# Down projection of the experts: weight columns held in TensorE, slots streamed, result transposed back before it is weighted

## Chip, cores and metric

The kernel runs on one core of one Trainium2 chip. The metric is the device time of one execution in microseconds (us). A core has a matrix engine (TensorE, PE), a vector engine (VectorE, DVE), a scalar engine (ScalarE, ACT), GpSimd (POOL), a queue for DMAs (SyncE, SP), and 16 DMA engines that all queues share. Each engine runs its own list of instructions in order and waits for the others at semaphores.

## What is computed

A tower of three parts: an edge filter on 32 images of 256 x 256, an attention block, and a mixture of experts. Only the last is touched. Its 8,224 tokens have 256 values each. Every token is routed to two of 32 experts, and an expert takes at most 321 tokens (its slots). Cut to what matters:

```python
idx = jnp.argsort(-score, axis=0)[:cap].T          # 32 experts x 321 slots
w = jnp.take_along_axis(Wc.T, idx, 1) * valid
xe = xf[idx]
up = jnp.einsum('eci,eji->ecj', xe, w_up)          # 256 -> 2 x 512
gate, upv = jnp.split(up, 2, axis=-1)
hact = jax.nn.silu(gate) * upv
ye = jnp.einsum('ecj,eoj->eco', hact, w_down)      # 512 -> 256
out = jnp.zeros((T, C), xf.dtype).at[idx.reshape(-1)].add((w[..., None] * ye).reshape(-1, C))
```

A small adapter (hidden width 128, one for two experts, factor 0.05) is added in the same way. The kernel appends it to the expert as a fifth block of 128 hidden values, so the down projection sums over 5 blocks.

## The kernel before

The expert stage is the last of the kernel. `body(n, r)` stands once per expert for each engine, with r = n mod 2 naming the buffer; experts 4 to 27 run in a loop of two bodies, the others are written out. All data are fp32; each operand is split into a high and a low part, and `mm3` (L243) makes one product from three matmuls (high x high, low x high, high x low). 322 slots (`CW`) are handled, in slot tiles of 128, 128 and 66 (`slot_tiles`, `ST` = 3).

For expert n the steps are:

- SP loads its weights into `raw` (L2078 up part, L2083 down part), once VectorE has finished with the buffer.
- ACT rounds them to `whi` in 4 pieces for the up part (`split_up`, L2190) and 2 for the down part (`split_down`, L2200), and VectorE makes the rest `wlo` (L2281).
- GpSimd gathers the token rows into `xe` (L2350, three indirect DMAs, one per slot tile). TensorE transposes them into `ps_f` (`turn`, L2151, six transpositions), ACT and VectorE make `xet` of it (L2220, L2298).
- `up(n, r, j)`, j = 0 to 4: 12 matmuls of 322 columns into `ps_s` (L247 to L249). ACT takes silu of one half (`gate`, L2180), VectorE multiplies it with the other (`hidden`, L2264 and L2266) and splits the product into `hs` (L2273, L2275).
- `down(m, r, st)`, one for each slot tile: the slots of `hs` are the stationary operand (128, 128 or 66 columns of it), the 256 weight columns stream through. 15 matmuls of 256 columns go into a bank of `ps_av`; its rows are slots. The tiles take the two banks in turn.
- `weigh` (L2211): ACT multiplies each row with the slot's weight and writes `ye`; GpSimd adds the rows into the output in HBM (L2366, an indirect DMA with add, one per slot tile).
- `row_weight` (L2288, L2289, L2291): three small VectorE instructions that make the slots' weights of expert n+1 in `weight[r]`. There are two such buffers, so it waits first:

```python
dve.wait_ge(xe_load[r], load_count(m, r, 16 * ST))
wait(dve, ye_done, ST * (m - 1))
```

With m = n+1 this is: all three weighings of expert n-1 are done. Behind it in VectorE's list stand the last piece of `wlo` of n+1 (`up_lo(n + 1, 1 - r, 3)`), for which `up(n + 1, r, 0)` waits on TensorE, and then the second down piece of n and `hidden` 4.

The down projection runs one expert late. TensorE's order in body n is: up 0, up 1, down tile 0 of n-1, up 2, down tile 1 of n-1, `turn` of n+1, up 3, down tile 2 of n-1, up 4. The last body (n = 32) has only `down_last`. GpSimd's order is fixed as well: for m = 0 to 31 the gathers of m+2, then the scatters of m. Hence the three gathers for n+2 stand behind the three scatters of n-1. They must have landed before `turn(n + 2)`, which TensorE reaches in body n+1.

Of the kernel before, what the change touches and what calls it, by code (L numbers as in the profile page):

```python
# [116 lines left out]
def build(nc, x, cls_rows, w1, b1uv, b1qk, w2, b2, gb, taps, r1w, r1s, r1m, r1b, r2w, wexp, consts, out,  # L117
# [9 lines left out]
    with ctx:  # L127
# [1894 lines left out]
        def s3(name, shape, dt=f32):  # L2022
            return experts.enter_context(nc.sbuf_tensor(name, shape, dt))
# [6 lines left out]
        xe = [s3(f"xe{i}", [P, ST, ROW]) for i in range(2)]  # L2030
        s3("over_raw", [P, POOL_COLS + 2 * WCOL - 4 * WCOL - 28 * CW - 2 * ST * ROW])
        ye = [s3(f"ye{i}", [P, ST, D]) for i in range(2)]
        sg = [s3(f"sg{i}", [P, CW]) for i in range(2)]
        hm = [s3(f"hm{i}", [P, CW]) for i in range(2)]
        weight = [s3(f"weight{i}", [P, ST]) for i in range(2)]
# [4 lines left out]


        w_hi_up, w_hi_dn, w_lo_up, w_lo_dn, xet_ps, xet_hi, xet_done = (sem(n) for n in ("w_hi_up", "w_hi_dn", "w_lo_up", "w_lo_dn", "xet_ps", "xet_hi", "xet_done"))
        up_ps, gate_act, h_done, h_hi, h_lo, down_ps, ye_done = (sem(n) for n in ("up_ps", "gate_act", "h_done", "h_hi", "h_lo", "down_ps", "ye_done"))
# [49 lines left out]
        def _(pe):  # L2093
# [17 lines left out]

            assert ST == 3

            def down_part(r, st, j0, j1):
                s0, w = slot_tiles[st]
                for j in range(j0, j1):
                    col = WDN + j * D
                    last = mm3(ps_av[(ST * r + st) % 2][0:w, 0:D], (hs[r][:, 0, j, s0:s0 + w], hs[r][:, 1, j, s0:s0 + w]),
                               (whi[r][:, col:col + D], wlo[r][:, col:col + D]), j == 0, j == 4)
                return last  # L2120

            def down(m, r, st):
                if not there(m):
                    return
                if st == 0:
                    pe.wait_ge(h_lo, 5 * m + 5)
                    pe.wait_ge(w_lo_dn, DNP * (m + 1))
                wait(pe, ye_done, ST * m + st - 1)
                down_part(r, st, 0, 5).then_inc(down_ps, 1)

            def down_last(m, r):

                pe.wait_ge(h_lo, 5 * m + 4)
                pe.wait_ge(w_lo_dn, DNP * (m + 1))
                wait(pe, ye_done, ST * m)
                down_part(r, 0, 0, 4)
                down_part(r, 1, 0, 4)
                pe.wait_ge(h_lo, 5 * m + 5)
                down_part(r, 0, 4, 5).then_inc(down_ps, 1)
                down_part(r, 1, 4, 5).then_inc(down_ps, 1)  # L2140
                pe.wait_ge(ye_done, ST * m + 1)
                down_part(r, 2, 0, 5).then_inc(down_ps, 1)

            def turn(m, r):
                if not there(m):
# [8 lines left out]
            def body(n, r):  # L2154
                if there(n):
                    up(n, r, 0)
                    up(n, r, 1)
                if isinstance(n, int) and n == NE:
                    down_last(n - 1, 1 - r)
                    return  # L2160
                down(n - 1, 1 - r, 0)
                if there(n):
                    up(n, r, 2)
                down(n - 1, 1 - r, 1)
                turn(n + 1, 1 - r)
                if there(n):
                    up(n, r, 3)
                down(n - 1, 1 - r, 2)
                if there(n):
                    up(n, r, 4)  # L2170

# [3 lines left out]
        def _(act):  # L2175
# [16 lines left out]
            def split_down(m, r, k):  # L2192

                if not there(m):
                    return
                if k == 0:
                    act.wait_ge(down_load[r], load_count(m, r, 16))
                    wait(act, down_ps, ST * (m - 1))
                lo, hi = dn_piece[k]
                nc.scalar.activation(whi[r][:, lo:hi], raw[r][:, lo:hi], ACT.Copy).then_inc(w_hi_dn, 1)  # L2200

            def weigh(m, r, st):
# [3 lines left out]
                if st == 0:  # L2206
                    act.wait_ge(w_ready, m + 1)
                    wait(act, added, 16 * ST * (m - 1))
                w = slot_tiles[st][1]
                act.wait_ge(down_ps, ST * m + st + 1)  # L2210
                nc.scalar.activation(ye[r][0:w, st, :], ps_av[(ST * r + st) % 2][0:w, 0:D], ACT.Copy,  # L2211
                                     scale=weight[r][0:w, st:st + 1]).then_inc(ye_done, 1)

            def turned_hi(m, r):
                if not there(m):
# [6 lines left out]
            def body(n, r):  # L2222
# [10 lines left out]
                if there(n):  # L2233
                    gate(n, r, 1)
                split_up(n + 1, 1 - r, 1)
                weigh(n - 1, 1 - r, 0)
                split_down(n, r, 0)
                if there(n):
                    gate(n, r, 2)
                split_up(n + 1, 1 - r, 2)  # L2240
                weigh(n - 1, 1 - r, 1)
                turned_hi(n + 1, 1 - r)
                if there(n):
                    gate(n, r, 3)
                split_up(n + 1, 1 - r, 3)
                weigh(n - 1, 1 - r, 2)
                split_down(n, r, 1)
                if there(n):
                    gate(n, r, 4)

# [3 lines left out]
        def _(dve):  # L2254
            def hidden(n, r, j):
# [4 lines left out]
                wait(dve, down_ps, ST * (n - 1))  # L2260
# [162 lines left out]
```

## Time and profile before

| what | value |
|---|---|
| median of 3 runs | 1458.1 us (1457.64 to 1460.12) |
| profiled execution | 1459.19 us, of which the span is 1457.4 us |
| mean granted TensorE clock | 0.936 of full speed |
| TensorE matmul busy | 1274.5 us (87% of the span) |
| VectorE busy | 1211.0 us (83%) |
| ScalarE busy | 892.6 us (61%) |
| GpSimd busy | 481.5 us (33%) |
| queue 1 (SP's loads and stores) | 153.80 MB, 35.9% of 16 engines' time |
| queue 0 (GpSimd's) | 21.25 MB, 9.1% |

The expert stage begins near 938 us with the first gathers and takes the rest of the span. The busy shares are means over all stages. What a step of the change is worth must be read from the order of events in one expert's period, and from what each engine waits for there. In the timelines a row is a start, a duration, the engine, the line, the operation and its operands; the duration of a matmul includes its way through the array, so matmuls follow each other faster than their durations say: the distance from start to start is the price. Brackets at the end of a row tell how long the engine was idle before, and who ended it.

### The profile page before, as it was taken

Reading aid. Unit: us, or ns where it says so; the run is one execution under the profiler, and the core shown is the slowest. Engines: PE = TensorE matmul, PEld = TensorE weight load, DVE = VectorE, ACT = ScalarE, POOL = GpSimd, SP = SyncE. Lnnn points to the kernel's source line nnn. Section 1 sums busy time; section 2 is a strip of 40 time slices with the busy share of each in tenths; the row PEclk is TensorE's granted clock in tenths of the full one; section 3 lists DMA queues with packets and bytes.
Section 4 is the critical chain, followed back from the end, with each engine's and each line's share of the span. In section 5 each row is a group of like instructions: output and inputs, shape, how many; then the busy total and the mean of one; then the engine's idle time right before and its main releaser. Section 6 shows DMA issues by size and latency. Waiting matters only on the chain. (4 is left out here: it accounts for less than half of the span.)

```text
span 1457.4 us, 33102 instructions
## 1 busy us (share of the span) xinstructions
PE 1274.5 (87%) x11891; PEld 1025.8 (70%) x11891; DVE 1211.0 (83%) x3133; ACT 892.6 (61%) x1608; POOL 481.5 (33%) x457
## 2 busy tenths in 40 slices
PE   3699999999999999999974342499999999999996
PEld 2467667667667667667653232399999999999996
DVE  4589999999999999999879878877777777777773
ACT  1377887887887887887772352545555555555552
POOL 0023233233233233232213000234554545555443
PEclk9799999999999999999996555699999999999999
DMA  8535445445445445442040600055565665655642
GB/s 243 136 94 133 112 116 133 111 116 133 110 118 133 112 116 133 113 116 58 31 145 17 93 0 0 20 189 153 163 191 152 179 178 148 188 169 150 198 123 24
DMA packets 128185, 176.69 MB, mean 121 GB/s; under 512 B 19946, under 2 KB 116476, under 8 KB 123964
## 3 DMA queue, kind: packets, MB, share of 16 engines
q1 hardware_dynamic: 110652, 153.80, 35.9%
q0 software_dynamic: 17408, 21.25, 9.1%
q8 instruction: 76, 1.25, 0.4%
q14 instruction: 49, 0.40, 0.1%
HBM read 133.85 MB, written 41.15 MB: 120 GB/s over the span
## 5 line engine op out<-in xcount | busy, mean ns | idle before, releaser
L796 ACT ACTIVATE at<-ps_s 128x1024 f32<-128x1024 f32 x256 | 248.3, 1027 | 5.5 <-PE ps_s L532 4.4
L2366 POOL DMA_INDIRECT out_rows<-ye,slot_token x96 | 152.3, 1587 | 227.2 <-ACT ye L2211 211.8
L247 PE MATMUL ps_s<-xet,whi 128*128 128x322 f32 x640 | 206.2, 322 | 11.0 <-DVE wlo L2281 9.5
L249 PE MATMUL ps_s<-xet,whi 128*128 128x322 f32 x640 | 199.4, 312 | 0.0
L248 PE MATMUL ps_s<-xet,wlo 128*128 128x322 f32 x640 | 198.9, 311 | 0.0
L2180 ACT ACTIVATE sg<-ps_s 128x322 f32<-128x322 f32 x160 | 70.5, 440 | 173.2 <-PE ps_s L249 132.9
L2281 DVE TENSOR_TENSOR wlo<-raw,whi 128x640 fp32r<-128x640 f32 x192 | 153.9, 817 | 2.3 <-ACT whi L2190 1.3
L2264 DVE TENSOR_TENSOR hm<-ps_s,sg 128x322 f32<-128x322 f32 x128 | 63.3, 494 | 98.8 <-ACT sg L2180 77.8
L548 PE MATMUL ps_av<-at,uv 128*16 128x257 f32 x2048 | 136.4, 384 | 1.0 <-ACT at L840 0.5
L247 PEld LDWEIGHTS ps_s<-xet,whi 128*128 128x128 f32 x640 | 121.7, 190 | 19.2 <-issue 15.7
L247 PE MATMUL ps_av<-whi,hs 128*128 128x256 f32 (+1 forms) x480 | 134.5, 280 | 0.6 <-issue 0.3
L248 PE MATMUL ps_av<-whi,hs 128*128 128x256 f32 (+1 forms) x480 | 134.5, 280 | 0.0
L249 PE MATMUL ps_av<-wlo,hs 128*128 128x256 f32 (+1 forms) x480 | 134.4, 280 | 0.0
L1527 POOL TENSOR_TENSOR rsa<-vea,n 128x2 f32<-128x2 f32 x32 | 22.3, 698 | 336.2 <-DVE vea L1042 336.2
L248 PEld LDWEIGHTS ps_s<-xet,wlo 128*128 128x128 f32 x640 | 121.6, 190 | 0.0
L249 PEld LDWEIGHTS ps_s<-xet,whi 128*128 128x128 f32 x640 | 121.6, 190 | 0.0
L2350 POOL DMA_INDIRECT xe<-token_rows,slot_token x96 | 102.9, 1072 | 30.2 <-issue 28.7
L532 PEld LDWEIGHTS ps_s<-qd,kd 32*128 32x128 f32 x2048 | 69.9, 185 | 44.2 <-issue 40.4
L532 PE MATMUL ps_s<-qd,kd 32*128 32x256 f32 x2048 | 96.1, 304 | 4.9 <-ACT at L796 2.5
L2190 ACT ACTIVATE whi<-raw 128x640 fp32r<-128x640 f32 x128 | 92.9, 731 | 11.9 <-PEq L2012 11.9
L2211 ACT ACTIVATE ye<-ps_av,weight 128x256 f32<-128x256 f32 (+1 forms) x96 | 45.3, 473 | 71.5 <-PE ps_av L249 70.8
L247 PE MATMUL ps_f<-xt,w1s 128*128 128x256 f32 x256 | 79.3, 310 | 6.1 <-DVE xt L1052 3.1
(393 smaller groups left out, 3556.5 us busy)
## 6 DMA issues: line engine op xcount, KB each, us to landing
raw<-in_wexp SPq DMA_DIRECT2D x32, 1280.0 KB, 6.4
halo<-gray_dram SPq DMA_DIRECT2D x96, 288.0 KB
xb<-in_x SPq DMA_DIRECT2D x64, 384.0 KB, 4.8
raw<-in_wexp SPq DMA_DIRECT2D x32, 640.0 KB
gray_dram<-g SPq DMA_DIRECT2D x32, 256.0 KB, 3.5
out_rows<-h SPq DMA_DIRECT2D x64, 128.0 KB, 3.3
token_rows<-xf SPq DMA_DIRECT2D x64, 128.0 KB, 2.5
pre_dram<-pre SPq DMA_DIRECT2D x30, 128.0 KB, 1.7
```

The source lines that it names most:

```text
L247: nc.tensor.matmul(o, lh, rh, start=first, stop=False)
L248: nc.tensor.matmul(o, ll, rh, start=False, stop=False)
L249: return nc.tensor.matmul(o, lh, rl, start=False, stop=last)
L532: last = nc.tensor.matmul(ps_s[j // 2][:, j % 2, kt, :], kd[r % 2][row, e, a, kt * 128:kt * 128 + 128], qd[r % 2][row, hl, e, a, :], start ...
L548: last = nc.tensor.matmul(o[32 * j:32 * j + 16, 0:R + 1], uv[r % 2][:, kt, 256 + h * 16:256 + h * 16 + 16], at[:, t, j, kt, 0:R + 1], star ...
L796: nc.scalar.activation(at[:, t, 2 * i:2 * i + 2, :, 0:R].rearrange("p j k q -> p (j k) q"), ps_s[i][:, :, :, :].rearrange("p j k q -> p (j ...
L2180: nc.scalar.activation(sg[b][:, :], ps_s[b][:, 0, :, :].rearrange("p k q -> p (k q)")[:, 0:CW], ACT.Silu).then_inc(gate_act, 1)
L2190: nc.scalar.activation(whi[r][:, lo:hi], raw[r][:, lo:hi], ACT.Copy).then_inc(w_hi_up, 1)
L2264: nc.vector.tensor_tensor(hm[b][:, :], o, sg[b][:, :], ALU.mult).then_inc(h_done, 1)
L2281: nc.vector.tensor_tensor(wlo[r][:, lo:hi], raw[r][:, lo:hi], whi[r][:, lo:hi].bitcast(f32), ALU.subtract).then_inc(done, 1)
L2350: nc.gpsimd.indirect_dma_start(out=xe[r][0:w, st, :], out_offset=None, in_=token_rows, in_offset=bass.IndirectOffsetOnAxis(ap=slot_token[0 ...
L2366: nc.gpsimd.indirect_dma_start(out=out, out_offset=bass.IndirectOffsetOnAxis(ap=slot_token[0:w, 3 * m + st:3 * m + st + 1], axis=0), in_=y ...
```

## The change

The roles in the down projection are exchanged. The weights become the stationary operand, 128 of their 256 output columns at a time (a half, `hf`), and all 322 slots stream through. That makes 2 x 15 matmuls of 322 columns per expert. Their result has output values as rows and slots as columns, so it cannot be weighted row by row. ACT first copies each half into a new SBUF tile `yt` (`keep_half`). TensorE turns it back with six transpositions into the same two `ps_av` banks (`back_rows`; two for each slot tile), and then ACT weighs as before.

In TensorE's order `down` 0 and 1 stand where tiles 0 and 1 stood, and `back_rows` where tile 2 stood. On ACT `keep_half` takes the places of weighings 0 and 1 (the first piece of `split_down` now stands ahead of it). All three weighings stand behind `gate` 3, `split_up` 3 and `split_down` 1. VectorE's and GpSimd's lists are the same. Nothing changes in the DMAs' sizes.

```diff
+        yt = s3("yt", [P, 2, CW])
...
-            def down_part(r, st, j0, j1):
-                s0, w = slot_tiles[st]
+            def down_part(r, hf, j0, j1):
                 for j in range(j0, j1):
-                    col = WDN + j * D
-                    last = mm3(ps_av[(ST * r + st) % 2][0:w, 0:D], (hs[r][:, 0, j, s0:s0 + w], hs[r][:, 1, j, s0:s0 + w]),
-                               (whi[r][:, col:col + D], wlo[r][:, col:col + D]), j == 0, j == 4)
+                    col = WDN + j * D + 128 * hf
+                    last = mm3(ps_av[hf][:, 0:CW], (whi[r][:, col:col + 128], wlo[r][:, col:col + 128]),
+                               (hs[r][:, 0, j, :], hs[r][:, 1, j, :]), j == 0, j == 4)
                 return last
 
-            def down(m, r, st):
+            def down(m, r, hf):
...
-                wait(pe, ye_done, ST * m + st - 1)
-                down_part(r, st, 0, 5).then_inc(down_ps, 1)
+                wait(pe, ye_done, ST * (m - 1) + 2 + hf)
+                down_part(r, hf, 0, 5).then_inc(down_ps, 1)
...
                 down_part(r, 0, 4, 5).then_inc(down_ps, 1)
                 down_part(r, 1, 4, 5).then_inc(down_ps, 1)
-                pe.wait_ge(ye_done, ST * m + 1)
-                down_part(r, 2, 0, 5).then_inc(down_ps, 1)
+
+            def back_rows(m):
+                if not there(m):
+                    return
+                pe.wait_ge(yt_done, 2 * m + 2)
+                for st, (s0, w) in enumerate(slot_tiles):
+                    for hf in range(2):
+                        last = nc.tensor.transpose(ps_av[st // 2][0:w, 256 * (st % 2) + 128 * hf:256 * (st % 2) + 128 * hf + 128],
+                                                   yt[:, hf, s0:s0 + w], ident)
+                    last.then_inc(back_ps, 1)
...
-                down(n - 1, 1 - r, 2)
+                back_rows(n - 1)
...
-                act.wait_ge(down_ps, ST * m + st + 1)
-                nc.scalar.activation(ye[r][0:w, st, :], ps_av[(ST * r + st) % 2][0:w, 0:D], ACT.Copy,
+                act.wait_ge(back_ps, ST * m + max(st + 1, 2))
+                nc.scalar.activation(ye[r][0:w, st, :], ps_av[st // 2][0:w, 256 * (st % 2):256 * (st % 2) + D], ACT.Copy,
                                      scale=weight[r][0:w, st:st + 1]).then_inc(ye_done, 1)
+
+            def keep_half(m, hf):
+
+                if not there(m):
+                    return
+                if hf == 0:
+                    wait(act, back_ps, ST * m)
+                act.wait_ge(down_ps, 2 * m + hf + 1)
+                nc.scalar.activation(yt[:, hf, :], ps_av[hf][:, 0:CW], ACT.Copy).then_inc(yt_done, 1)
...
-                weigh(n - 1, 1 - r, 0)
                 split_down(n, r, 0)
+                keep_half(n - 1, 0)
...
-                weigh(n - 1, 1 - r, 1)
+                keep_half(n - 1, 1)
...
-                weigh(n - 1, 1 - r, 2)
                 split_down(n, r, 1)
+                for st in range(ST):
+                    weigh(n - 1, 1 - r, st)
```

Where the instructions stand now. TensorE of the kernel before, at the end of up 3 and through the third tile's down projection to the start of up 4 (`ps_s` is up, `ps_av` is down):

```order
L247 MATMUL ps_s<-xet1,whi1 128x322
L248 MATMUL ps_s<-xet1,wlo1 128x322
L249 MATMUL ps_s<-xet1,whi1 128x322
L247 MATMUL ps_av0<-whi0,hs0 66x256 [waits ye_done]
L248 MATMUL ps_av0<-whi0,hs0 66x256
L249 MATMUL ps_av0<-wlo0,hs0 66x256
...
L247 MATMUL ps_s<-xet1,whi1 128x322 [waits h_done]
```

Four more such triples stand at the dots. The same place in the changed kernel:

```order
L247 MATMUL ps_s<-xet1,whi1 128x322
L248 MATMUL ps_s<-xet1,wlo1 128x322
L249 MATMUL ps_s<-xet1,whi1 128x322
L2149 MATMUL ps_av0<-cst,yt 128x128 [waits yt_done]
L2149 MATMUL ps_av0<-cst,yt 128x128 x3
L2149 MATMUL ps_av1<-cst,yt 66x128 x2
L247 MATMUL ps_s<-xet1,whi1 128x322 [waits h_done]
```

The 15 matmuls of the third tile have gone, and the six transpositions of `yt` stand between up 3 and up 4.

ScalarE of the kernel before, from `gate` 3 (`sg1`) to `gate` 4 (`sg0`) of one expert:

```order
L2180 ACTIVATE sg1<-ps_s 128x322 [waits h_done,up_ps]
L2190 ACTIVATE whi1<-raw1 128x640
L2210 REGISTER_ALU
L2211 ACTIVATE ye1<-ps_av1,weight1 66x256 [waits down_ps]
L2200 ACTIVATE whi0<-raw0 128x640
L2177 REGISTER_ALU
L2180 ACTIVATE sg0<-ps_s 128x322 [waits h_done,up_ps]
```

And in the changed kernel:

```order
L2190 ACTIVATE sg1<-ps_s 128x322 [waits h_done,up_ps]
L2200 ACTIVATE whi1<-raw1 128x640
L2210 ACTIVATE whi0<-raw0 128x640
L241 ISA [waits w_ready]
L2220 REGISTER_ALU [waits added]
L2221 ACTIVATE ye1<-ps_av0,weight1 128x256 [waits back_ps] x2
L2220 REGISTER_ALU
L2221 ACTIVATE ye1<-ps_av1,weight1 66x256 [waits back_ps]
L2187 REGISTER_ALU
L2190 ACTIVATE sg0<-ps_s 128x322 [waits h_done,up_ps]
```

All three weighings (`ye`) now stand behind both pieces of weights (`whi`); only the third stood between these two gates before, ahead of the down piece.

## Rows read from the trace of the kernel before

**Rows 1.** Timeline of GpSimd: scatters (`out_rows`) and gathers (`xe`), start and duration.

```profile
966.75 2.13 POOL L2366 DMA_INDIRECT out_rows<-ye,slot_token  x1 [14.33 <-ACT ye L2211]
...
1106.43 1.73 POOL L2366 DMA_INDIRECT out_rows<-ye,slot_token  x1 [2.66 <-ACT ye L2211]
...
1113.61 1.48 POOL L2366 DMA_INDIRECT out_rows<-ye,slot_token  x1 [2.59 <-ACT ye L2211]
1115.40 1.10 POOL L2350 DMA_INDIRECT xe<-token_rows,slot_token  x1 [0.30 <-issue]
...
1118.16 1.02 POOL L2350 DMA_INDIRECT xe<-token_rows,slot_token  x1 [0.30 <-issue]
...
1417.44 1.64 POOL L2366 DMA_INDIRECT out_rows<-ye,slot_token  x1 [2.63 <-ACT ye L2211]
...
1445.26 1.59 POOL L2366 DMA_INDIRECT out_rows<-ye,slot_token  x1 [4.59 <-ACT ye L2211]
...
1449.02 1.48 POOL L2366 DMA_INDIRECT out_rows<-ye,slot_token  x1 [0.30 <-issue]
```

**Rows 2.** Table by stretch: length, busy time per engine, PEclk, DMA share, GB/s.

```profile
1100.00:1200.00 100.00, 97.95 (x723) 96.21 (x722) 77.50 (x169) 52.15 (x104) 51.88 (x40) 1.00 0.63 181
...
1108.00:1109.00 1.00, 1.00 (x12) 1.00 (x11) 0.97 (x3) 0.31 (x1) 0.16 (x1) 1.00 0.45 19
...
905.00:910.00 5.00, 0.00 (x0) 0.00 (x0) 4.76 (x18) 0.00 (x0) 0.00 (x0) 0.56 0.00 2
...
1385.00:1390.00 5.00, 4.16 (x34) 3.95 (x33) 2.85 (x6) 2.26 (x5) 2.79 (x2) 1.00 0.42 70
...
1386.00:1386.50 0.50, 0.50 (x6) 0.49 (x5) 0.50 (x1) 0.02 (x1) 0.20 (x1) 1.00 0.12 41
```

**Rows 3.** Timeline of TensorE from `turn` to the next expert's first matmul.

```profile
1108.49 0.72 PE L2151 MATMUL ps_f<-cst,xe 128*128 128x128 f32 x6
1109.02 0.39 PE L247 MATMUL ps_s<-xet,whi 128*128 128x322 f32 x1
...
1110.88 0.28 PE L247 MATMUL ps_av<-whi,hs 128*66 128x256 f32 x1
...
1112.64 0.31 PE L247 MATMUL ps_s<-xet,whi 128*128 128x322 f32 x1
...
1114.27 0.31 PE L249 MATMUL ps_s<-xet,whi 128*128 128x322 f32 x1
1114.91 0.41 PE L247 MATMUL ps_s<-xet,whi 128*128 128x322 f32 x1 [0.33 <-DVE wlo L2281]
```

**Rows 4.** Timeline of VectorE: `row_weight` begins, and the last up piece follows.

```profile
1113.46 0.22 DVE L2288 SCALAR_TENSOR_TENSOR is<-xe,cst 128x3 f32<-128x3 f32 x1
...
1113.96 1.56 DVE L2281 TENSOR_TENSOR wlo<-raw,whi 128x640 fp32r<-128x640 f32 x2
```

**Rows 5.** Timeline of ScalarE: four pieces in a row, one expert, two weighings in a row.

```profile
939.78 2.60 ACT L2190 ACTIVATE whi<-raw 128x640 fp32r<-128x640 f32 x4
...
1111.08 0.44 ACT L2180 ACTIVATE sg<-ps_s 128x322 f32<-128x322 f32 x1 [1.26 <-PE ps_s L249]
1111.41 0.73 ACT L2190 ACTIVATE whi<-raw 128x640 fp32r<-128x640 f32 x1
1112.84 0.47 ACT L2211 ACTIVATE ye<-ps_av,weight 66x256 f32<-66x256 f32 x1 [0.70 <-PE ps_av L249]
...
1444.01 0.84 ACT L2211 ACTIVATE ye<-ps_av,weight 128x256 f32<-128x256 f32 x2 [3.40 <-PE ps_av L249]
```

**Rows 6.** Timelines of GpSimd and TensorE: third gather, and `turn` that waits for gathers.

```profile
942.26 1.18 POOL L2350 DMA_INDIRECT xe<-token_rows,slot_token  x1 [0.30 <-issue]
...
945.17 1.33 PE L2151 MATMUL ps_f<-cst,xe 128*128 128x128 f32 x6 [9.81 <-DMA xe<-token_rows,slot_token]
...
1380.88 1.02 POOL L2350 DMA_INDIRECT xe<-token_rows,slot_token  x1 [0.30 <-issue]
...
1387.53 0.78 PE L2151 MATMUL ps_f<-cst,xe 128*128 128x128 f32 x6 [0.84 <-DMA xe<-token_rows,slot_token]
```

**Rows 7.** DMA queues from 1000 to 1400 us: packets, MB, share of 16 engines.

```profile
q1 hardware_dynamic: 7394, 50.72, 32.8%
q0 software_dynamic: 14019, 17.01, 27.0%
```

More of the change, by code:

```diff
@@ L2042, in build @@
         w_hi_up, w_hi_dn, w_lo_up, w_lo_dn, xet_ps, xet_hi, xet_done = (sem(n) for n in ("w_hi_up", "w_hi_dn", "w_lo_up", "w_lo_dn", "xet_ps", "xet_hi", "xet_done"))
-        up_ps, gate_act, h_done, h_hi, h_lo, down_ps, ye_done = (sem(n) for n in ("up_ps", "gate_act", "h_done", "h_hi", "h_lo", "down_ps", "ye_done"))
+        up_ps, gate_act, h_done, h_hi, h_lo, down_ps, yt_done, back_ps, ye_done = (sem(n) for n in (
+            "up_ps", "gate_act", "h_done", "h_hi", "h_lo", "down_ps", "yt_done", "back_ps", "ye_done"))
         w_part, w_ready, added, tail_clear = (sem(n) for n in ("w_part", "w_ready", "added", "tail_clear"))
@@ L2112, in _ @@
             assert ST == 3
-            def down_part(r, st, j0, j1):
-                s0, w = slot_tiles[st]
+            def down_part(r, hf, j0, j1):
                 for j in range(j0, j1):
-                    col = WDN + j * D
-                    last = mm3(ps_av[(ST * r + st) % 2][0:w, 0:D], (hs[r][:, 0, j, s0:s0 + w], hs[r][:, 1, j, s0:s0 + w]),
-                               (whi[r][:, col:col + D], wlo[r][:, col:col + D]), j == 0, j == 4)
+                    col = WDN + j * D + 128 * hf
+                    last = mm3(ps_av[hf][:, 0:CW], (whi[r][:, col:col + 128], wlo[r][:, col:col + 128]),
+                               (hs[r][:, 0, j, :], hs[r][:, 1, j, :]), j == 0, j == 4)
                 return last
-            def down(m, r, st):
+            def down(m, r, hf):
                 if not there(m):
                     return
-                if st == 0:
+                if hf == 0:
                     pe.wait_ge(h_lo, 5 * m + 5)
                     pe.wait_ge(w_lo_dn, DNP * (m + 1))
-                wait(pe, ye_done, ST * m + st - 1)
-                down_part(r, st, 0, 5).then_inc(down_ps, 1)
+                wait(pe, ye_done, ST * (m - 1) + 2 + hf)
+                down_part(r, hf, 0, 5).then_inc(down_ps, 1)
             def down_last(m, r):
@@ L2134, in down_last @@
                 pe.wait_ge(w_lo_dn, DNP * (m + 1))
-                wait(pe, ye_done, ST * m)
+                pe.wait_ge(ye_done, ST * m)
                 down_part(r, 0, 0, 4)
@@ L2167, in body @@
                     up(n, r, 3)
-                down(n - 1, 1 - r, 2)
+                back_rows(n - 1)
                 if there(n):
@@ L2197, in split_down @@
                     act.wait_ge(down_load[r], load_count(m, r, 16))
-                    wait(act, down_ps, ST * (m - 1))
+                    wait(act, down_ps, 2 * (m - 1))
                 lo, hi = dn_piece[k]
@@ L2209, in weigh @@
                 w = slot_tiles[st][1]
-                act.wait_ge(down_ps, ST * m + st + 1)
-                nc.scalar.activation(ye[r][0:w, st, :], ps_av[(ST * r + st) % 2][0:w, 0:D], ACT.Copy,
+                act.wait_ge(back_ps, ST * m + max(st + 1, 2))
+                nc.scalar.activation(ye[r][0:w, st, :], ps_av[st // 2][0:w, 256 * (st % 2):256 * (st % 2) + D], ACT.Copy,
                                      scale=weight[r][0:w, st:st + 1]).then_inc(ye_done, 1)
+            def keep_half(m, hf):
+                if not there(m):
+                    return
+                if hf == 0:
+                    wait(act, back_ps, ST * m)
+                act.wait_ge(down_ps, 2 * m + hf + 1)
+                nc.scalar.activation(yt[:, hf, :], ps_av[hf][:, 0:CW], ACT.Copy).then_inc(yt_done, 1)
             def turned_hi(m, r):
@@ L2259, in hidden @@
                 dve.wait_ge(gate_act, 5 * n + j + 1)
-                wait(dve, down_ps, ST * (n - 1))
+                wait(dve, down_ps, 2 * (n - 1))
                 o = ps_s[b][:, 1, :, :].rearrange("p k q -> p (k q)")[:, 0:CW]
```

## The prediction

> **What bounds the kernel now.** I read the views in the order of the groups. The expert stage runs from 966 us to 1425 us with one expert after another: the first scatters of experts 0 and 29 start at 966.75 and 1417.44 us, 29 periods, so one period is 450.69/29 = 15.54 us [rows 1]. TensorE looks like the bound, 97.95 us busy of 100 at a granted clock of 1.00 [rows 2]. But it waits in every period: its last matmul of an expert starts at 1114.27, its first of the next at 1114.91, released by `wlo` of VectorE [rows 3]. So TensorE and a loop through VectorE are nearly level. In that loop `gate` 3 (ACT, 1111.08) lets VectorE make `hm`, split a piece, then do `row_weight` (1113.46) and the last up piece `wlo` (1113.96), and TensorE may begin [rows 4, 5]. `row_weight` of expert n+1 overwrites the row weights that expert n-1 used, so by its wait on `ye_done` it may not start before the third weighing of n-1. That one ran from 1112.84 to 1113.31, 0.15 us before `row_weight` started: it was just in time [rows 4, 5].
>
> A third loop runs through GpSimd. Its order is fixed: three scatters of expert n-1, then three gathers for n+2. The gathers must land before the transpositions of `turn` in the next expert. At 1387.53 TensorE sat waiting for just that, 6.65 us after the third gather's issue began at 1380.88 [rows 6]. That loop has next to no room either.
>
> I put all times of one expert relative to G, the start of `gate` 3 (1111.08 in these rows).
>
> **The change on TensorE.** Removed are 45 matmuls of 256 columns; 15 of them take 1112.64 - 1110.88 = 1.76 us, so 0.117 each and 5.28 us in all [rows 3]. Added are 30 of 322 columns; the up projection has this shape, 11 of them in 1114.27 - 1112.64 = 1.63 us, so 0.148 each and 4.44 us [rows 3]. The six transpositions back have the form of the six in `turn`, which take 1109.02 - 1108.49 = 0.53 us [rows 3]. Sum: 4.44 + 0.53 - 5.28 = -0.31 us per expert, 10 us in 32. For bounds I take 0.53 to 0.8 us for the six.
>
> The Trainium skill ("TensorE: Matmul & The Clock Gate", Part 4: PE-mode transpose) gives about 275 ns for one transposition in a kernel's context. By that six would cost 1.65 us and TensorE alone would be 0.8 us per expert slower. The trace speaks against it as a price in a row of them: six in 0.53 us.
>
> That saving is real but stands in the wrong place. Ahead of G, two tiles (30 x 0.117 = 3.52 us) become two halves (4.44 us): +0.92 us on every loop through G. Behind G, 1.76 us of the third tile become 0.53 us, and that stretch ended in a wait already. So all of the saving falls where TensorE waits anyway.
>
> **The change on ScalarE and VectorE.** Two copies `keep_half` are added, one of them in place of each of the first two weighings, which is where ACT waited anyway. They cost nothing while ACT waits there 0.7 us and more; with that cover gone, about 0.4 us each. All three weighings now stand behind `gate` 3, a piece of `split_up` and a piece of `split_down`. The up piece starts 0.33 us after the gate; pieces in a row follow each other by (2.60 - 0.73)/3 = 0.62 us, so the down piece starts at G + 0.95 and the first weighing at G + 1.57; two weighings in a row take 0.84 us, one 0.47, so they follow by 0.37 and the third starts at G + 2.31 and ends at G + 2.78 [rows 5]. The transpositions are done by about G + 0.8, so they are not what it waits for. `row_weight` follows by 0.03 to 0.15 us: G + 2.93 against 1113.46 - 1111.08 = 2.38 before, +0.55 us (bounds 0.43 and 0.6) [rows 4, 5]. Queued behind it on VectorE is the last up piece, and TensorE waits for that. The cover on TensorE behind G is 0.53 + 12 x 0.148 = 2.3 us, so the gap at the next expert's start grows from 0.3 to about 2.1 us. **This loop's period: 15.54 + 0.92 + 0.55 = 17.0 us.**
>
> **The change on GpSimd and its queue.** Before, the three scatters were spread over the period; only the third (1113.61, G + 2.5) stood close ahead of the gathers, whose third began at 1118.16 (G + 7.1) [rows 1]. Now all three wait for weighings behind G. The first weighing ends at G + 2.04. At the end of the kernel the weighing ended at 1444.48 and the first scatter began at 1445.26, 0.78 later; the third followed at 1449.02, 3.76 later [rows 1, 5]. So: first scatter G + 2.82, third G + 6.58, first gather 1.79 later (1115.40 - 1113.61), third gather another 2.76 later: G + 11.13, 4.0 us later than before [rows 1]. Then it lands after a time L, `turn` may start, and from there to the next G it is 1111.08 - 1108.49 = 2.59 us [rows 3, 5]. **This loop's period: 11.13 + L + 2.59 = 13.72 + L.**
>
> L is not shown for this order. Lower bound: 2.91 us with the queues nearly empty (942.26 to 945.17); upper bound: 6.65 us beside a whole load of weights [rows 6]. Between them I count the DMA engines' work. Weights and software queue take 32.8% and 27.0% of 400 us over 26 experts, 9.2 us of all 16 engines per expert [rows 7]. Before, two of the three scatters were issued before G, ahead of the weights. Now none is. A scatter's packets come about 2.1 us after its start (1106.43; the engines' share in 1108 to 1109 is 0.45 [rows 1, 2]), so from G + 4.95 everything runs in one piece: scatters, the weights that `wlo` releases, gathers last in their queue. They end at G + 4.95 + 9.2 = G + 14.15. At 1386 to 1386.5 the engines were down to 0.12 and TensorE started at 1387.53, so 1.4 us from the last packet to the wait's end [rows 2, 6]. `turn` starts at G + 15.55, which is L = 4.4, near the middle of the two rows. **Period 18.15 us**; that is more than 17.0, so this loop rules, 2.6 us per period over 15.54.
>
> **Sum.** 30 experts (1 to 30) have both a predecessor to scatter and a successor to prepare: 30 x 2.6 = 78 us. At the end the first scatter waits for both halves, a copy and the transpositions: 4.44 + 0.44 + 0.53 against 3.52 = +1.9 us. Together 80 us on the profiled execution's 1459.2 us (span 1457.4): 1539 us. The median of the runs is 1458.1, 1.1 lower, so 1538 us.
>
> **Rivals.**
> 1. *Only the VectorE loop counts* (gathers land in time). For it: L = 2.91 would give 16.6, under 17.0. Against it: three scatters, weights and gathers now meet in the DMA engines. Price 30 x 1.47 + 2 = 46 us: 1504 us. The Trainium skill ("DMA: Bandwidth & Descriptors", Anatomy of one DMA — SWDGE (gpsimd) path) prices such a DMA at 2.0 us plus its bytes over 436 GB/s; for 66 rows that is an estimate of 2.2 us and would put the case here. The trace shows 2.91 and 6.65 us. Chance 0.20.
> 2. *The queue is as slow as beside a full load*: L = 5.5 to 6.65, periods 19.2 to 20.4, 1570 to 1605 us. For it: in the rows with long L there were fewer scatters in the queue than now. Against it: the weights are issued about 4 us ahead of the first gather, so most of them are through. Chance 0.09 beyond the range.
> 3. *TensorE's own sum rules, faster*: the weights loop and the gathers turn out to have room, each period loses 0.31 us: 1448 us. It decides only if `row_weight` does not wait for the third weighing and the gathers not for the scatters. The waits stand in the code. Chance 0.04.
> 4. *The clock falls* in the new gaps (about 2.1 us at an expert's start, 1.1 at `turn`). With TensorE idle for all of 905 to 910 it was granted 0.56; around the 0.84 us wait before 1387.53 it was 1.00 [rows 2, 6]. If the 12 matmuls after one of the gaps ran at half speed it would be 1.8 us more per period, about 1590 us. Chance 0.03.
>
> **Chances and range.** My forecast, the GpSimd loop at 17.3 to 19.2 us per period (1513 to 1570 us), has 0.64. The range holds it and the first rival: 1498 to 1572 us. A measurement of this kernel can tell about 0.2% from no change; slower by more 0.94, faster by more 0.04, within 0.02 (taken from the lower end of rival 1).
>
> **What the profile after would show.** Scatters in threes 1.9 us apart, starting near G + 2.8, the third gather near G + 11; waits of 1 to 2 us of `turn` on the DMA of `xe` in most experts (if they are missing, rival 1 holds); the wait of an expert's first matmul on `wlo` at 1.5 to 2.2 us; 30 matmuls for the down projection at 0.148; clock 1.00. I would be wrong if scatter packets overlap with weights at little cost (then 1504 to 1520), or if ACT reached the weighings much earlier than G + 1.6.

## The result, and the profile after

The changed kernel takes 1519.4 us (median of 3 runs, 1518.14 to 1520.4) against 1458.1: ratio 1.0421, 95% interval 1.0407 to 1.0434. It is slower by 61 us; 80 were forecast. Its profiled execution has a span of 1518.6 us.

From the page of the changed kernel, to be read beside the page of before:

```profile
span 1518.6 us, 32669 instructions
...
PE 1279.4 (84%) x11603; PEld 1028.1 (68%) x11603; DVE 1221.8 (80%) x3133; ACT 908.4 (60%) x1672; POOL 486.7 (32%) x457
...
q1 hardware_dynamic: 110652, 153.80, 33.9%
q0 software_dynamic: 17408, 21.25, 7.8%
```

Where does one period begin and end? GpSimd's timeline of the changed kernel, one expert. It answers to [rows 1]. `gate` 3, my G, starts at 1114.98 here:

```profile
1109.48 1.02 POOL L2370 DMA_INDIRECT xe<-token_rows,slot_token  x1 [0.30 <-issue]
1117.86 1.64 POOL L2386 DMA_INDIRECT out_rows<-ye,slot_token  x1 [7.36 <-ACT ye L2221]
1119.80 1.60 POOL L2386 DMA_INDIRECT out_rows<-ye,slot_token  x1 [0.30 <-issue]
1121.71 1.49 POOL L2386 DMA_INDIRECT out_rows<-ye,slot_token  x1 [0.31 <-issue]
1123.51 1.10 POOL L2370 DMA_INDIRECT xe<-token_rows,slot_token  x1 [0.30 <-issue]
...
1126.38 1.02 POOL L2370 DMA_INDIRECT xe<-token_rows,slot_token  x1 [0.30 <-issue]
```

The three scatters now stand together, ahead of the three gathers. The first scatter starts at G + 2.88 and the third gather at G + 11.40. The first scatters of experts 0 and 29 start at 973.50 and 1483.36, so the mean period is 509.86/29 = 17.58 us, against 15.54 before. The shortest periods are 16.8 to 16.9; others go up to 18.9. The 29 periods account for 59.2 us of the 61.2 us between the two spans. The remaining 2.0 lie at the stage's two ends.

The stretches of [rows 2] again (columns as there: stretch, its length, busy time of the five engines, granted clock, share of the DMA engines, GB/s):

```profile
1082.00:1084.00 2.00, 0.15 (x2) 0.00 (x0) 1.51 (x6) 0.85 (x3) 1.36 (x1) 1.00 0.00 0
1084.00:1088.00 4.00, 3.86 (x16) 3.87 (x17) 2.27 (x4) 0.30 (x1) 3.34 (x3) 0.57 0.85 220
...
1100.00:1200.00 100.00, 87.84 (x601) 85.47 (x600) 72.96 (x154) 49.34 (x106) 48.03 (x36) 1.00 0.52 158
1000.00:1400.00 400.00, 348.90 (x2338) 339.27 (x2337) 283.23 (x596) 195.29 (x413) 183.76 (x138) 0.98 0.50 151
```

TensorE is busy for 87.84 of 100 us where it was 97.95 [rows 2]. The idle time is told by the list of waits of the changed kernel, 1000 to 1400 us (the engine and what it works on, what ended the wait; sum in us, count, longest; `PEld` is TensorE's loading of the stationary operand):

```profile
PE ps_s L247 <- DVE wlo L2301: 45.5, 23, 2.0
...
DVE is L2308 <- ACT ye L2221: 10.4, 23, 0.5
...
PEld ps_f L2160 <- DMA xe<-token_rows,slot_token: 8.7, 13, 1.5
...
PE ps_f L2160 <- DMA xe<-token_rows,slot_token: 5.6, 8, 1.3
```

The first line holds one wait of 1.98 us in each of 23 experts. That is the gap at an expert's start, 0.33 us in [rows 3]. The second shows why: `row_weight` now waits 0.45 us for the third weighing. The last two lines are `turn` waiting for gathers; on the matmul side it does so in 8 of 23 experts, by up to 1.3 us.

The order around G, which answers to [rows 3 to 5]. First ScalarE, then VectorE, then TensorE:

```profile
1114.98 0.44 ACT L2190 ACTIVATE sg<-ps_s 128x322 f32<-128x322 f32 x1 [1.35 <-PE ps_s L249]
1115.32 0.73 ACT L2200 ACTIVATE whi<-raw 128x640 fp32r<-128x640 f32 x1
1115.94 0.73 ACT L2210 ACTIVATE whi<-raw 128x640 fp32r<-128x640 f32 x1
1116.57 1.18 ACT L2221 ACTIVATE ye<-ps_av,weight 128x256 f32<-128x256 f32 x3
```

```profile
1117.90 0.22 DVE L2308 SCALAR_TENSOR_TENSOR is<-xe,cst 128x3 f32<-128x3 f32 x1 [0.46 <-ACT ye L2221]
```

```profile
1114.78 0.82 PE L2149 MATMUL ps_av<-cst,yt 128*128 128x128 f32 x6
1115.35 0.40 PE L247 MATMUL ps_s<-xet,whi 128*128 128x322 f32 x1
...
1117.06 0.31 PE L249 MATMUL ps_s<-xet,whi 128*128 128x322 f32 x1
1119.36 0.41 PE L247 MATMUL ps_s<-xet,whi 128*128 128x322 f32 x1 [1.99 <-DVE wlo L2301]
```

The weighings start at G + 1.59 and end at G + 2.77; `row_weight` starts at G + 2.92. TensorE does its six transpositions back in 0.57 us, ends what it has, and stands still until `wlo` comes.

### The profile page after: what moved, and what is told of

Same layout as the page of the kernel before. It is cut to its first block and busy times, and to the rows that moved or that the text cites. A ratio compares the mean times of both kernels' runs of the same rounds, so it can differ in the third digit from the quotient of the medians.

```text
span 1518.6 us, 32669 instructions
## 1 busy us (share of the span) xinstructions
PE 1279.4 (84%) x11603; PEld 1028.1 (68%) x11603; DVE 1221.8 (80%) x3133; ACT 908.4 (60%) x1672; POOL 486.7 (32%) x457
## 5 line engine op out<-in xcount | busy, mean ns | idle before, releaser
L247 PE MATMUL ps_s<-xet,whi 128*128 128x322 f32 x640 | 213.6, 334 | 59.9 <-DVE wlo L2301 58.5
L249 PE MATMUL ps_s<-xet,whi 128*128 128x322 f32 x640 | 204.1, 319 | 0.0
L248 PE MATMUL ps_s<-xet,wlo 128*128 128x322 f32 x640 | 203.4, 318 | 0.0
L247 PEld LDWEIGHTS ps_s<-xet,whi 128*128 128x128 f32 x640 | 125.8, 197 | 68.2 <-issue 55.1
L248 PEld LDWEIGHTS ps_s<-xet,wlo 128*128 128x128 f32 x640 | 125.9, 197 | 0.0
L249 PEld LDWEIGHTS ps_s<-xet,whi 128*128 128x128 f32 x640 | 125.7, 196 | 0.0
L247 PE MATMUL ps_av<-hs,whi 128*128 128x322 f32 x320 | 99.4, 311 | 0.3 <-DVE wlo L2301 0.3
L248 PE MATMUL ps_av<-hs,wlo 128*128 128x322 f32 x320 | 99.3, 310 | 0.0
L249 PE MATMUL ps_av<-hs,whi 128*128 128x322 f32 x320 | 99.2, 310 | 0.0
L2295 DVE TENSOR_TENSOR hs<-hm,hs 128x322 fp32r<-128x322 f32 x160 | 79.2, 495 | 5.5
```

The lines of the kernel that those rows point to most:

```text
L247: nc.tensor.matmul(o, lh, rh, start=first, stop=False)
L248: nc.tensor.matmul(o, ll, rh, start=False, stop=False)
L249: return nc.tensor.matmul(o, lh, rl, start=False, stop=last)
L2295: nc.vector.tensor_tensor(hs[r][:, 1, j, :], hm[b][:, :], hs[r][:, 0, j, :].bitcast(f32), ALU.subtract).then_inc(h_lo, 1)
```

## The experiments

Each kernel was timed over three rounds beside the kernel before, on the same chip (medians of before: 1456.2 us for a_gather_first, a_weight_later, a_both and a_fill, 1457.7 for the others). "Period" is the mean distance of the first scatters of experts 0 to 29.

**Theory after the result.** Three things stack: a loop through VectorE of 16.86 us, late gathers in some experts, and TensorE's clock, which falls behind some of the gaps. Rivals: one of them alone explains the rest, or the waits only cover one another.

### Gathers ahead of scatters: a_gather_first

```
@@ GpSimd's loop
             gather(1)
+            gather(2)
             for m in range(NE):
-                gather(m + 2)
+                gather(m + 3)
                 wait(pool, added, 16 * ST * m)
```

> The changed kernel with one edit on GpSimd: the three gathers of an expert stand ahead of the scatters that they stood behind (three gathers are issued before the loop, then m+3 instead of m+2). Theory 1 (the loop through the third weighing, row_weight and the last up piece sets a floor of about 16.9 us per expert; gathers that land late add 0 to 1.3 us in about half of the experts, lower clock behind the new gap about 1.5 us in a quarter): only the gather waits vanish, 9 to 16 us in all, so 1503 to 1511 us; no wait of turn on the DMA of xe is left, the waits of an expert's first matmul on wlo stay at 2.0 us. Theory 2 (the loop through the scatters and gathers rules, as forecast): the period falls from 17.6 to the VectorE loop's 16.9 in every expert, 1498 to 1502 us, since slow blocks would have been hidden in that loop. If neither holds and the queue costs nothing, 1519 us.

Measured: 1507.3 us, ratio 1.0344 (1.0322 to 1.0367). No wait of `turn` is left. The gap stays, as the list of waits of this kernel shows for the same 400 us, and the stretch below it still has a granted clock of 0.98:

```profile
PE ps_s L247 <- DVE wlo L2301: 45.4, 23, 2.0
```

```profile
1000.00:1400.00 400.00, 354.63 (x2398) 348.21 (x2397) 290.22 (x609) 198.35 (x422) 187.46 (x141) 0.98 0.52 155
```

The periods alternate between 16.77 and 16.86 us, but every sixth is 18.36 to 18.39. So late gathers cost 11 to 12 us of the 61 (by ratio and by median; the ratio's interval is 3 us either way), the VectorE loop is the floor, and something else adds 1.5 us in every sixth expert.

### Matmuls that keep TensorE busy in the gap: a_fill

Twelve matmuls of 322 columns are added to the changed kernel; nothing uses their result.

```
                 if j == 0:
-                    pe.wait_ge(w_lo_up, UPP * (n + 1))
                     pe.wait_ge(xet_done, n + 1)
+                    for _k in range(12):
+                        nc.tensor.matmul(ps_f[0][:, 0:CW], xet[r][:, 0, 0, 0:128], xet[r][:, 0, 0, :], start=True, stop=True)
+                    pe.wait_ge(w_lo_up, UPP * (n + 1))
```

> The changed kernel with 12 matmuls of 322 columns more per expert in TensorE's gap ahead of up 0, behind its wait on xet and ahead of its wait on wlo; they write a PSUM bank that is free then and nothing reads them, so the output is the same. They take 1.77 us of a gap of 2.0 us. Theory 1 (the clock falls to its lower level behind the gap in some experts and costs up to 1.5 us there): no up block at 0.27 us per matmul is left, granted clock 1.00 throughout the stage, about 10 us less, 1506 to 1513 us; late gathers take some of that back. Rival (the clock plays no part, slow blocks come from elsewhere, for instance operands or DMA traffic): the same or more, 1519 to 1525 us.

Measured: 1509.8 us, 1.0369 (1.0351 to 1.0387), 8 to 10 us faster than the changed kernel with more work on TensorE. Its stretch:

```profile
1000.00:1400.00 400.00, 391.56 (x2667) 381.33 (x2666) 288.41 (x607) 199.07 (x420) 186.69 (x140) 1.00 0.51 154
```

The granted clock is 1.00 where it was 0.98. What such a fall costs can be seen in TensorE's timeline of the changed kernel:

```profile
1084.14 0.49 PE L247 MATMUL ps_s<-xet,whi 128*128 128x322 f32 x1 [1.99 <-DVE wlo L2301]
1084.43 0.47 PE L248 MATMUL ps_s<-xet,wlo 128*128 128x322 f32 x1
...
1087.38 0.47 PE L247 MATMUL ps_s<-xet,whi 128*128 128x322 f32 x1
...
1087.84 0.31 PE L249 MATMUL ps_s<-xet,whi 128*128 128x322 f32 x1
1087.99 0.31 PE L247 MATMUL ps_s<-xet,whi 128*128 128x322 f32 x1
```

From 1084.43 to 1087.38 lie 11 matmuls, 0.268 us each; at full clock they are 0.148 [rows 3]. Over 12 to 13 matmuls that is the 1.5 us of a long period. The granted clock of 1084 to 1088 is 0.57 in the row above: near the lower of its two levels, 1.2 of 2.4 GHz.

### The row weights behind the last up piece: a_weight_later

```
                 hidden_lo(n, r, 3)
+                up_lo(n + 1, 1 - r, 3)
                 if there(n + 1):
                     row_weight(n + 1, 1 - r)
-                up_lo(n + 1, 1 - r, 3)
```

> The changed kernel with one edit on VectorE: row_weight stands behind the last up piece of wlo instead of ahead of it, so TensorE's next expert no longer waits for the third weighing. Theory 1: the gap at an expert's start shrinks from 2.0 to 1.0 us and the clock stays up, but the gathers still stand behind the scatters, the third one starting 11.4 us behind gate 3 and landing 2.9 to 4.2 us later: a period of 16.8 to 17.5 us, 1500 to 1515 us, with waits of turn on xe of 1 us and more in nearly all experts. Rival (only the VectorE loop counts): 16.9 - 1.1 = 15.8 us per expert, 1468 to 1475 us.

Measured: 1509.8 us, 1.0363 (1.0343 to 1.0383). The list of waits shows what took the place of the gap:

```profile
PEld ps_f L2160 <- DMA xe<-token_rows,slot_token: 32.0, 23, 3.2
...
PE ps_f L2160 <- DMA xe<-token_rows,slot_token: 25.9, 23, 3.0
...
PE ps_s L247 <- DVE wlo L2301: 21.4, 23, 1.0
```

The gap shrinks from 1.98 to 0.93 us per expert, and `turn` now waits in all 23, 1.1 us each. Only 8 to 10 us are won (by ratio and by median), since the period falls to 17.0 in most experts and stops there: that is the loop through GpSimd. By the timelines of this kernel the third gather starts at G + 11.63, `turn` 2.73 us behind it, and the next G 2.64 us behind `turn` (the middle values of all experts): 17.0. So this loop is as long as VectorE's although the gathers land quickly, in 2.6 to 3.0 us in all experts but one.

The clock was expected to stay up, and it fell twice, each time behind a long wait of `turn` (2.13 and 2.96 us). Here is the second, with the stretch behind it:

```profile
1212.88 0.78 PE L2160 MATMUL ps_f<-cst,xe 128*128 128x128 f32 x6 [2.96 <-DMA xe<-token_rows,slot_token]
```

```profile
1213.50:1216.50 3.00, 3.00 (x14) 2.98 (x13) 0.89 (x2) 0.68 (x2) 0.00 (x0) 0.55 0.00 0
```

### Both: a_both

The edits of a_gather_first and a_weight_later together.

> The changed kernel with both edits: gathers ahead of the scatters, row_weight behind the last up piece. Theory 1: both new loops are open. What is left is gate 3, one product, one piece, one split and the last up piece on VectorE (3.3 us behind gate 3) and 12.35 us from an expert's first matmul to gate 3: 15.65 us per expert, 1460 to 1466 us, still 0.9 us of wait on wlo per expert, clock 1.00. Rival (TensorE's sum of 14.8 to 15.1 us per expert rules once the waits are gone): 1440 to 1450 us. If ScalarE's added copies or the transpositions cost something that I do not see: over 1475 us.

Measured: 1467.1 us, 1.0072 (1.0054 to 1.0090), period 15.79; no wait for gathers, clock 1.00, gap 0.94. The two edits win 12 and 10 us alone and 52 together. That is what two loops of nearly one length look like: 16.8 to 16.9 us through VectorE, 17.0 through GpSimd, and 15.79 with both opened. Some of the surplus is the clock's, which fell in six experts of a_gather_first, at 1.5 us each, and in none here. Expected were 1460 to 1466; the last 0.14 us per period were not traced.

### Weighings at the end, with the matmuls of before: b_late_weigh

The kernel before, its three tiles of matmuls kept, but all three weighings at the end of ScalarE's step. For this, tiles 0 and 1 share a bank.

```
                 split_up(n + 1, 1 - r, 1)
-                weigh(n - 1, 1 - r, 0)
...
                 split_up(n + 1, 1 - r, 2)
-                weigh(n - 1, 1 - r, 1)
...
                 split_up(n + 1, 1 - r, 3)
-                weigh(n - 1, 1 - r, 2)
                 split_down(n, r, 1)
+                for st in range(ST):
+                    weigh(n - 1, 1 - r, st)
```

> The kernel before, with its own down projection (three slot tiles, 45 matmuls of 256 columns), but with all three weighings behind gate 3, the up piece and the down piece, as in the changed kernel. For that tiles 0 and 1 lie in the two halves of one PSUM bank. This is the place of the weighings without the exchanged matmuls. Theory 1 (the place of the weighings is what costs): row_weight comes 0.55 us later, a VectorE loop of 16.1 us; the gathers stand behind three scatters, third gather 11.3 us behind gate 3, a GpSimd loop of 16.8 to 17.2 us, which rules: 1495 to 1508 us, waits of turn on xe of 0.5 to 1.2 us in nearly all experts, no fall of the clock. Rival (the 0.92 us that the halves are longer ahead of gate 3 is needed for the loss, the queue is not): 1474 to 1480 us.

Measured: 1513.5 us, 1.0382 (1.0359 to 1.0404), period 17.26. Its waits, same stretch:

```profile
PE ps_f L2148 <- DMA xe<-token_rows,slot_token: 24.3, 24, 2.8
PE ps_s L247 <- DVE wlo L2277: 20.3, 23, 0.9
```

So the place of the weighings alone, with no stationary weights, no halves and no transpositions, costs 56 us, nearly as much as the whole change. TensorE's list of waits in this stretch has none on the shared bank. I was 5 us or more too low on its size: `turn` waits for gathers in every expert here, 1.0 us on average, at clock 1.00. It is the loop through GpSimd that rules in this kernel.

### The two edits on the kernel before: b_weight_later, b_both

b_weight_later is the kernel before with the row weights behind the last up piece; b_both also has the gathers ahead of the scatters.

> The kernel before with only row_weight behind the last up piece of wlo. If the wait on wlo (0.33 us idle in every period) was the larger part of what the two edits gave together (15.54 to 14.90 us per expert), about 15.1 us and 1444 to 1450 us; if the gathers' place was needed as well, because TensorE arrives at turn earlier and then waits for xe, 1452 to 1457 us with such waits of 0.3 us and more in most experts.

> The kernel before with gathers ahead of the scatters and row_weight behind the last up piece. Theory 1: the last up piece is ready 0.5 us earlier, which is what TensorE waited for; its own sum rules, 15.1 to 15.2 us per expert against 15.54: 1443 to 1448 us; no wait on wlo and none on xe is left. It stands against the changed kernel with the same two edits (1467.1 us, 15.78 us per expert): with both loops open, what the exchanged matmuls cost is their place ahead of gate 3. Rival (the scatters' and gathers' place and row_weight meant nothing in the kernel before): 1455 to 1459 us.

Measured: 1448.6 us, 0.9938 (0.9920 to 0.9956), and 1438.6 us, 0.9871 (0.9854 to 0.9888), period 14.90. In b_both no wait on `wlo` or `xe` is left and TensorE is busy for 400 of 400 us: there it is the bound at last. The first lies in its 1444 to 1450, the second is better than its 1443 to 1448. Before the change, then, each loop already took something: 9 us and 10 us. With the same two edits a_both takes 28 us more than b_both: that is what the change still costs when these two waits are out of the way.

### Weighings directly behind gate 3: a_weigh_first

```
+                for st in range(ST):
+                    weigh(n - 1, 1 - r, st)
                 split_up(n + 1, 1 - r, 3)
                 split_down(n, r, 1)
-                for st in range(ST):
-                    weigh(n - 1, 1 - r, st)
```

> The changed kernel with one edit on ScalarE: the three weighings stand directly behind gate 3, ahead of the up piece and the down piece. Theory 1: the first weighing starts when the transpositions are done, about 0.5 us behind gate 3 instead of 1.59, the third ends 1.1 us earlier than now, so row_weight waits for nothing (VectorE loop 16.3 us) and the third gather starts 10.3 us behind gate 3 (GpSimd loop 15.7 to 17.0 us): 16.3 to 16.7 us per expert, 1482 to 1495 us. Rival (the number of scatters in one row, not the time of the weighings, sets the gathers' landing): 1510 to 1519 us.

Measured: 1516.2 us, 1.0415 (1.0385 to 1.0444). This was a clear miss; the time is the one that the rival gave. GpSimd's timeline and the `turn` that follows, in this kernel:

```profile
1109.71 1.71 POOL L2386 DMA_INDIRECT out_rows<-ye,slot_token  x1 [7.25 <-ACT ye L2221]
1111.72 2.13 POOL L2386 DMA_INDIRECT out_rows<-ye,slot_token  x1 [0.30 <-issue]
1114.15 1.49 POOL L2386 DMA_INDIRECT out_rows<-ye,slot_token  x1 [0.30 <-issue]
...
1118.84 1.02 POOL L2370 DMA_INDIRECT xe<-token_rows,slot_token  x1 [0.30 <-issue]
```

```profile
1123.51 0.78 PE L2160 MATMUL ps_f<-cst,xe 128*128 128x128 f32 x6 [1.65 <-DMA xe<-token_rows,slot_token]
```

The scatters start at G + 1.74, 1.1 us earlier than in the changed kernel, but the third gather only 0.5 earlier (G + 10.87), and it needs 4.67 us to land. That is this kernel's longest landing, but `turn` waits in all 24 experts of the 400 us, 0.84 us on average. What was won in front was lost in the issue of the scatters and in the transfer. SyncE issues the up weights at G + 3.87 here and at G + 4.41 in the changed kernel, so in both they meet scatters and gathers, and I asked whether they are what the gathers wait behind.

### Weights loaded later: a_weights_after

In the changed kernel, SyncE's load of the next up weights waits for `turn` instead of for `wlo`.

```
-                    wait(sp, w_lo_up, UPP * (m - 1))
+                    wait(sp, xet_ps, 2 * m)
```

> The changed kernel with one edit on SyncE: the load of an expert's up weights waits until turn of the expert before it is done (xet_ps) instead of the last up piece. So two thirds of the weights' bytes are moved out of the stretch in which scatters and gathers run; they still land before they are needed. GpSimd's order is the changed kernel's. Theory A (the gathers land late because the DMA engines are full of weights and scatters together): the third gather lands about 2.9 us after its issue began, no wait of turn on xe is left, and the time is that of gathers put first, 1503 to 1508 us, with the slow clock block in one expert of five or so. Theory B (the landing is set by GpSimd's issue behind three scatters, 11.4 us behind gate 3): the waits of turn stay, 1512 us or more.

Measured: 1508.7 us, 1.0347 (1.0328 to 1.0365), just above the 1503 to 1508 of theory A. The clock is no better: eight experts run part of their way at the lower level, against seven in the changed kernel. Of the waits for gathers (8 on the matmul side, 13 on the weight side, in the changed kernel's 400 us) one each is left:

```profile
PE ps_f L2160 <- DMA xe<-token_rows,slot_token: 1.3, 1, 1.3
```

The scatters are as many and stand where they stood (the third gather starts at G + 11.4 as before); only the weights moved. So the late landing needs the weights in the same microseconds: neither the scatters alone make it, nor GpSimd's time to issue them. How the DMA engines divide themselves between the two queues was not traced.

### Weighings and gathers both early: a_weigh_gather_first

> The changed kernel with two edits: weighings directly behind gate 3 (which alone gave 1516 us, with the waits of turn on xe grown to 1 to 1.6 us), and gathers ahead of the scatters. If the VectorE loop is what the weighings' place lengthens by 0.55 us, it is now 16.86 - 0.54 = 16.3 us in every expert, the gap ahead of up 0 1.45 us instead of 1.99, and no gather waits: 1482 to 1490 us, 1480 to 1485 if the clock stays up behind the shorter gap. Rival (up pieces that come 1.1 us later on ScalarE hold VectorE's last piece back instead): 1500 us or more.

Measured: 1481.5 us, 1.0167 (1.0148 to 1.0185), period 16.29, a gap of 1.43 us in each expert, clock 1.00 throughout, no long period. With the gathers out of the way the weighings' earlier end is worth what a_weigh_first was expected to show: 16.86 - 16.29 = 0.57 us per expert, the 0.55 of the forecast.

### The same arithmetic in another order: a_reordered

The changed kernel with its steps moved so that nothing new ends late: the second half of the down projection behind up piece 3, `back_rows` behind up piece 4, the weighings behind `gate` 4, the row weights last on VectorE, gathers ahead of scatters.

```
@@ TensorE
-                down(n - 1, 1 - r, 1)
                 turn(n + 1, 1 - r)
                 if there(n):
                     up(n, r, 3)
-                back_rows(n - 1)
+                down(n - 1, 1 - r, 1)
                 if there(n):
                     up(n, r, 4)
+                back_rows(n - 1)
```

> The changed kernel with its new parts in other places. TensorE: turn, up 3, then half 1, up 4, and the transpositions back last. ScalarE: the second keep_half behind the down piece, the weighings behind gate 4. VectorE: row_weight last in the body. GpSimd: gathers ahead of the scatters. Theory 1: half 1 (2.22 us) leaves the stretch ahead of gate 3 and fills TensorE's gap behind it; the VectorE loop falls to 10.1 + 3.4 = 13.5 us and TensorE's own sum rules: 60 x 0.148 + 30 x 0.148 + 2 x 0.53 = 14.4 us and up to 0.4 us of joints, 14.6 to 14.9 us per expert, 1431 to 1441 us, faster than the kernel before and than it with the two edits. Rival (the down projection with slots streaming is no cheaper on TensorE, for instance by PSUM or by the transpositions): 1446 us or more.

Measured: 1433.0 us, 0.9825 (0.9804 to 0.9845), faster than both kernels. Its stretch:

```profile
1000.00:1400.00 400.00, 400.00 (x2795) 399.36 (x2794) 325.94 (x714) 236.99 (x493) 222.33 (x160) 1.00 0.60 174
```

TensorE is the bound, at a period of 14.63 us against 14.90 in b_both, which has the matmuls of before with its own waits gone. The difference, 0.28 us before rounding, is the saving of the new down projection, where 0.31 had been worked out. It appears once TensorE is what everything waits for.

## Why the prediction was right and where it was not

- **TensorE's sum, -0.31 us per expert**: confirmed as -0.28 (a_reordered against b_both). The half's 15 matmuls take 0.148 us each and six transpositions back 0.57 (0.53 forecast). That the saving stands in the wrong place was right too: in the changed kernel it ends in the gap.
- **VectorE loop, 17.0 us**: about 16.86 measured, in the shortest periods of the changed kernel and nearly all of a_gather_first. `row_weight` came at G + 2.92 (forecast 2.93); the way from the first matmul to the next G grew by 0.77 us instead of 0.92: it is 16.86 - 4.38 = 12.48 now, 15.54 - 3.83 = 11.71 before [rows 1, 3, 5]. This part is 29 x 1.32 = 38 us of the 61.
- **GpSimd's order**: first scatter G + 2.88 (2.82), third gather G + 11.40 (11.13). Right, and 0.3 us of the gathers' lateness was missed.
- **The step that failed: the landing, L = 4.4 us**, and with it the period of 18.15. I took the DMA engines' work as one piece with the gathers at its end. In the changed kernel the third gather of the expert above starts at 1126.38 and `turn` at 1129.25 without any wait, so L was 2.87 at most, just under what I had called its lower bound. Where `turn` waits, in ten experts, L is 2.7 to 4.5 us, as here (the third gather and the `turn` of another expert):

```profile
1212.82 1.02 POOL L2370 DMA_INDIRECT xe<-token_rows,slot_token  x1 [0.30 <-issue]
```

```profile
1215.55 0.78 PE L2160 MATMUL ps_f<-cst,xe 128*128 128x128 f32 x6 [1.28 <-DMA xe<-token_rows,slot_token]
```

  With L = 2.73 the loop through GpSimd is 11.4 + 2.73 + 2.64 = 16.8 us: level with VectorE's, not 1.15 us above it. The mechanism is real (a_gather_first, a_weights_after), its size is not: this loop costs 11 to 12 us beside the other, not 1.15 us in each of 30 experts. The DMA engines' piece of work in the expert above can be read from its stretches:

```profile
1119.50:1120.00 0.50, 0.50 (x4) 0.50 (x5) 0.50 (x2) 0.00 (x0) 0.20 (x1) 1.00 0.00 0
1120.00:1128.00 8.00, 8.00 (x56) 8.00 (x55) 5.82 (x12) 3.98 (x8) 6.19 (x5) 1.00 1.04 319
1128.00:1128.50 0.50, 0.50 (x5) 0.50 (x4) 0.50 (x2) 0.29 (x1) 0.00 (x0) 1.00 0.55 145
1128.50:1129.00 0.50, 0.50 (x6) 0.50 (x5) 0.50 (x2) 0.00 (x0) 0.00 (x0) 1.00 0.05 17
```

  One piece it is, and it begins at G + 5.0 (forecast 4.95). But it ends near G + 13.3 instead of 14.15, and `turn` follows at G + 14.27, about 1.0 us later at most, where I had 1.4. Part of the over-count can be seen in the queues of the changed kernel, 1000 to 1400 us, against [rows 7]:

```profile
q1 hardware_dynamic: 6562, 44.91, 28.8%
q0 software_dynamic: 12511, 15.27, 21.4%
```

  With 22.8 experts in 400 us, the weights take 5.05 us per expert as before, but the software queue 3.8 instead of 4.2. Why is not shown: in a_weights_after the scatters and gathers are bunched in the same way, and with 23.0 experts in 400 us the queue takes 4.2 us again:

```profile
q0 software_dynamic: 12651, 15.59, 24.4%
```

- **The clock** had 3 chances in 100 as a rival at 1590 us. It did fall, but in about one expert of four or five rather than in each: 1.5 us a time (I had worked out 1.8 for a fall), 8 to 10 us in all (a_fill). This error is opposite to that of the landing and hid part of it: without the falls the result would have been near 1510.
- **The ends**: +2.0 us, 1.9 forecast.

Sum by the changed kernel's own trace: 38 (VectorE loop) + 29 x (17.58 - 16.86) = 21 (gathers and clock) + 2 = 61 us. The two edits that take out one of the 21's parts each win 11 to 12 and 8 to 10. Rival 1, with 1504 us, was the nearer description of what rules. The mean period of 17.58 us lies among the 17.3 to 19.2 of my forecast, but mostly for another reason than the one given, and in part by luck: the falls of the clock, to which I had given 3 chances in 100, brought 8 to 10 us of it. The warning at the prediction's end, 1504 to 1520 if scatter packets overlap at little cost, is where it came out.

What stays open: why some experts' gathers land within 2.9 us and others, with the same order, not; and why the clock falls in one expert and not in its neighbour with the same gap.

## What to carry to other kernels

Where two loops are nearly level, ask of a saving not how large it is but behind which wait it falls; and if the step that is made cheaper also ends later, list everything that reads its end, down to the queue that it feeds. Moving three evacuations to the end of a step bunched three scatters in front of three gathers and cost 56 us by itself, while the saved matmuls were worth 6 us (1438.6 against 1433.0) and were to be had only after the order was mended on three engines. When two waits cover each other, try both cures together: alone they won 12 and 10 us, together 52.

## What the runs showed of the hardware that I had not expected

- TensorE's granted clock fell to its lower level behind gaps of 1.99 us that came once in each period of about 17 us: in every sixth expert of a_gather_first, irregularly in the changed kernel. Between the gaps of a_gather_first TensorE was busy. In a_weight_later, with gaps of 0.93 us, it fell behind waits of `turn` of 2.13 and 2.96 us. Gaps of 1.43 us (a_weigh_gather_first) and 0.94 us (a_both) left it at 1.00, and so did 12 matmuls of unused result placed in the 1.99 us gap (a_fill). A fall behind the gap cost 1.5 us, over 12 to 13 matmuls at 0.268 us.
- The time from the start of the last gather to its landing was at most 2.87 us in some experts of the changed kernel, 2.7 to 4.5 in others, and up to 4.67 in a_weigh_first. Loading the weights later took all but one of the changed kernel's waits in 400 us away.
- The issue of the scatters was slower in a_weigh_first: the second began 2.01 us after the first and the third 2.43 after that, against 1.94 and 1.91 in the changed kernel. The weights alone do not explain it, since a_weights_after, which loads them at another time, has the distances of the changed kernel. The cause is open.
